# Retention stage of an eight-batch hybrid network: a ScalarE copy, a VectorE product and the key projection change places

## The reference, cut to what matters

```python
qkv = h @ weight_quant(qkv_w).T                 # q, k, v: 16 heads x 16
scores = einsum('bhtd,bhsd,hts->bhts', q, k, mask)   # mask: exp(-s*(t-s)), causal
o = 0.25 * einsum('bhts,bhsd->bhtd', scores, v)      # (chunked in the reference)
out = rmsnorm(rmsnorm(o) ) @ weight_quant(proj_w).T
x = x + out
```

## Time and profile before

| what | us |
|---|---|
| median of the runs | 1151.98 |
| lowest run | 1150.12 |
| profiled execution, its time | 1146.32 |
| profiled execution, its span | 1144.5 |
| PE busy in the span | 928.1 (81%) |
| DVE busy in the span | 703.6 (61%) |
| ACT busy in the span | 368.4 (32%) |

### The profile page before, as it was taken

The page is one execution under the profiler, slowest core; times in us unless marked ns, Lnnn a source line. Parts: engine busy times, 40 slices in busy tenths (PEclk is TensorE's granted clock), DMA queues, the critical chain, the costliest instruction groups (busy, mean ns, idle before and its releaser), DMA issues.

```text
span 1144.5 us, 21028 instructions
## 1 busy us (share of the span) xinstructions
PE 928.1 (81%) x8018; PEld 782.6 (68%) x8018; DVE 703.6 (61%) x1291; ACT 368.4 (32%) x663; POOL 320.1 (28%) x352
## 2 busy tenths in 40 slices
PE   3589987775886887778877999999668885699998
PEld 2466665454765776655655899997556664699998
DVE  4458876544577868788776545445676657454443
ACT  2126554331412321234332523233222222232222
POOL 4202221014845666321201104010044633330000
PEclk9669998686889998998887999999877878799999
DMA  8745541000011000355450000011454544210000
GB/s 220 231 126 154 156 117 44 2 1 10 19 56 47 1 1 1 112 170 153 127 166 14 1 2 1 1 44 41 89 96 87 110 84 74 37 20 19 11 20 19
DMA packets 148581, 76.78 MB, mean 67 GB/s; under 512 B 108993, under 2 KB 139713, under 8 KB 148481
## 3 DMA queue, kind: packets, MB, share of 16 engines
q1 hardware_dynamic: 139376, 65.47, 22.8%
q0 software_dynamic: 1424, 4.98, 1.5%
q10 hardware_dynamic: 7680, 4.98, 1.5%
HBM read 45.77 MB, written 29.36 MB: 66 GB/s over the span
## 4 chain that ended last, share of the span: by engine, by line
PE 56%; DVE 25%; issue 7%; ACT 5%; POOL 3%; SPq 2%; DMA 1%; DVEq 0%; ACTq 0%; POOLq 0%
PE SC L386 16%; PE pb L386 8%; PE OT L386 7%; DVE mx L1322 3%; PE OT L2154 3%; PE pa L386 3%; PE OT L1891 3%; PE SC L1844 3%; PE OT L2068 2%; PE SC L1873 2%; PE SC L2142 2%; PE pa L2337 2%; DVE pr L1575 2%; DVE m L1573 2%; DVE pr L1571 2%
## 5 line engine op out<-in xcount | busy, mean ns | idle before, releaser
L386 PE MATMUL SC<-xT_h,w_h 128*128 128x256 f32 x512 | 147.7, 289 | 13.8 <-DVE xT_l L1734 11.5
L386 PE MATMUL SC<-xT_l,w_h 128*128 128x256 f32 x512 | 146.1, 285 | 0.0
L386 PE MATMUL SC<-xT_h,w_l 128*128 128x256 f32 x512 | 145.3, 284 | 0.0
L386 PEld LDWEIGHTS SC<-xT_h,w_h 128*128 128x128 f32 x512 | 98.1, 192 | 17.0 <-DVE xT_l L1734 15.1
L1322 DVE TENSOR_REDUCE mx<-SC 128x4 f32<-128x1024 f32 x64 | 78.1, 1221 | 46.1 <-PE SC L1844 45.7
L386 PE MATMUL OT<-w,Qs 128*128 128x256 f32 x768 | 103.0, 283 | 2.3 <-DVE Qs L1744 1.4
L386 PEld LDWEIGHTS SC<-xT_h,w_l 128*128 128x128 f32 x512 | 98.2, 192 | 0.0
L386 PEld LDWEIGHTS OT<-w,Qs 128*128 128x128 f32 x768 | 95.2, 189 | 3.7 <-issue 2.1
L386 PEld LDWEIGHTS SC<-xT_l,w_h 128*128 128x128 f32 x512 | 97.7, 191 | 0.0
L1740 DVE TENSOR_TENSOR hidden_f<-SC,silu_gate 128x512 f32<-128x512 f32 x64 | 44.1, 689 | 84.5 <-ACT silu_gate L1202 84.5
L1744 DVE TENSOR_TENSOR Qs<-hidden_f,Qs 128x512 fp32r<-128x512 f32 x64 | 45.0, 703 | 44.7 <-ACT Qs L1210 44.7
(11 more groups left out here) (424 smaller groups left out, 2645.0 us busy)
## 6 DMA issues: line engine op xcount, KB each, us to landing
Qs<-q_stack SPq DMA_DIRECT2D x56, 128.0 KB, 2.8
k_stack<-KT_h SPq DMA_DIRECT2D x16, 256.0 KB, 2.6
k_stack<-KT_l SPq DMA_DIRECT2D x16, 256.0 KB, 3.1
q_stack<-QT_h SPq DMA_DIRECT2D x16, 256.0 KB, 2.2
q_stack<-QT_l SPq DMA_DIRECT2D x16, 256.0 KB, 2.8
o_groups<-b_O ACTq DMA_DIRECT2D x8, 512.0 KB, 2.9
Qs<-q_stack SPq DMA_DIRECT2D x56, 64.0 KB, 2.9
Ks<-k_stack SPq DMA_DIRECT2D x28, 128.0 KB, 3.2
```

The costliest lines, as they stand in the source:

```text
L386: ins = pe.matmul(out_ap, left[a], right[b], start=first and n == 0, stop=last and n == len(terms) - 1, **more)
```

## The change

On ACT, `x_high` goes from behind `squares`, `a_high` and the copies to the head of the round. On DVE, `a_low` goes from ahead of `masked` to behind `masked` and `x_low`. The key projection `k_out`, its high part `k_high`, its low part `low(b, KT, ...)` and its `store` each go one round later. Nothing is added or taken away, and no wait is changed.

```diff
@@ SP, narrow, at_slot
                                 for b in due(g, -12):
                                     store(b, "ql", "qstore", "qload", QT, q_dram)
-                                for b in due(g, -10):
+                                for b in due(g, -9):
                                     store(b, "kl", "kstore", "kload", KT, k_dram)
@@ ACT, narrow, at_slot
                     if ret:
+                        for b in due(g, -15):
+                            x_high(b)
                         for b in due(g, -8):
                             v_out(b)
...
                         for b in due(g, 26):
                             a_high(b)
-                        for b in due(g, -15):
-                            x_high(b)
                         for b in due(g, -13):
                             q_high(b)
-                        for b in due(g, -11):
+                        for b in due(g, -10):
                             k_high(b)
@@ DVE, narrow, at_slot
                     if ret:
-                        for b in due(g, 26):
-                            a_low(b)
                         for b, r in running(g, 0):
                             masked(b, r)
                         for b in due(g, -15):
                             x_low(b)
+                        for b in due(g, 26):
+                            a_low(b)
                         for b in due(g, -12):
                             low(b, QT, pb, "qh", "ql")
-                        for b in due(g, -10):
+                        for b in due(g, -9):
                             low(b, KT, pa, "kh", "kl")
```

## The result

The changed kernel takes 1140.51 us (median of four runs, 1134.99 to 1141.2) against 1151.35: a ratio of 0.9899, 95% interval 0.9859 to 0.9939, so 11 us or 1% less. The forecast was 1142. A few runs of the kernel before, of e4 and of e13 took 1231.97 us or more and are left out of the ratios. The run times go with the granted clock: of 56 later runs of the kernel before (1141.01 to 1159.82 us, median 1149.9), five with a mean clock of 0.885 took 1148.08 to 1150.26 us, and four at 0.893 took 1141.31 to 1141.71.

What follows compares the result with a forecast made beforehand. Neither engine is full; stalls between PE and DVE take 2.28 us a cycle. Gains 7.0 + 0 + 2.1 = 9.1 us off the profiled 1146.3 give 1137.2; 4.7 added for higher-lying runs gives 1142, range 1132 to 1154.

Steps and rivals of the forecast that it cites:

- Key projection: Retention cycles, rounds 5 to 7: moving it one round later gains 1.39 us a cycle, 7.0 in five; ends 0 and 11.4.
- residual stall: DVE before masked 7: the idle time shrinks from 1.76 to 0.36 us, since `k_out` now stands before round 7's scores.
- `store` and the loads: SP's queue: storing keys one round, about 2 us, later comes out of some 10 us of slack; cost nothing.
- One step of the layout: End of the laid-out cycle: `to_tokens` starts 0.28 us after `residual`, at 572.87; DVE is last, 574.46 against 575.85.
- The two orders: `x_high` ahead on ACT, `a_low` behind masked product on DVE: zero; ends 1.1 us gain, 2.8 loss.
- Clock: TensorE's granted clock in cycles 2 and 3: half of 4.24 us comes back, 2.1; ends 0 and 4.2.
- Lead-in and batch 0: Two key projections ahead of batch 0, among other layers' work: nothing, with ends of 0.9 us either way.
- What would show it: Changed profile: `k_out`'s 9.4 us wait, idle before masked 6 and `x_low`'s waits gone; full-clock cycles about 15.7 us; higher clock.
- The first: Rival, rounds 6 and 7: the stall only moves; gain 0 to 4 us, about 1150; chance 0.22.
- The second: Rival: DVE becomes the bound, all stalls go and the clock stays up; 15.6 us gain, 1135; chance 0.11.
- The third: Rival, `pa`'s rotation: late `x_turned` holds up `x_high`, `out_high` and round 2's `attend`; 10.6 us slower, 1162; chance 0.09.

Runs made afterwards that it cites:

- e4: Kernel before, with round 6's scores computed three more times ahead of `k_out` in cycles 1 to 5: 1139.09 us, ratio 0.9917.
- e13: e12 with `x_high` back in its old place, `a_low` still behind the masked product: 1138.64 us, ratio 0.992.
- e1: Kernel before with only the key projection, its copies and store one round later, both orders as before: 1142.74 us, ratio 0.995.
- e2: Kernel before with only `x_high` ahead and `a_low` behind, keys in their old round: median 1147.41 us, six runs from 1127.08 to 1150.87.
- e5: Kernel before with only the keys of batches 3 and later one round later, both orders as before: 1140.78 us, ratio 0.9911.
- e3: Changed kernel with the keys of batches 0 to 2 in their old round: 1136.37 us, ratio 0.9885.
- e12: The same kernel as e6, run again on another chip: 1126.95 us, ratio 0.9826.
- e11: Kernel before, unedited, profiled a second time on the same chip as e10: 1152.74 us, one run.
- e9: Kernel before with only `k_out` moved behind round 6's scores on PE; copies, low part and store as before: 1151.7 us, ratio 1.0026.
- e10: Changed kernel, unedited, profiled a second time on the same chip as e11: 1143.49 us, one run.
- e8: e3 with round 4's scores computed two more times ahead of `q_out` in cycles 3 to 5: 1131.44 us, ratio 0.9829.
- e6: Changed kernel with only the keys of batches 0 and 1 in their old round: 1126.72 us, ratio 0.9806.
- second pair: Second profiles of the changed kernel (e10) and the kernel before (e11), both unedited, on one chip: 1143.49 and 1152.74 us.

## Why the prediction came out as it did

The total held (1142 against 1140.51), in part by luck: the clock gave 5.7 us more than forecast, and the lead-in and batch 0 took 6.7 that the sum did not have. The two nearly cancelled.

**Key projection.** Right. Laid out at 1.39 us a cycle, it measured 1.37 alone (e1's cycle 3, at full clock). Taking it five times is a little much: between e2 and the changed kernel, at full clock in both, cycles 2 to 5 give 1.77, 1.50, 1.50 and only 0.51. The residual stall, laid out at 0.36 before masked 7, is 0.40. That `store` and the loads have the slack held: no scores wait for a load. One step of the layout counts unlike ends: `to_tokens` is set 0.28 us behind the recorded end of `residual` (573.32 for 0.74 us), while every other end is the start of what follows; with the recorded end the two chains come out within 0.01 us of each other, and the gain stays.

**The two orders.** Priced at nothing, with an end of 1.1 us of gain: mis-sized. In a full-clock cycle the price of nothing is nearly right: alone they give 0.1 us (e2), beside late keys 0.2 to 0.3 (15.53 against e1's 15.75, e5 against e3): with DVE busy 14.66 of 15.53 us there is little else that it waits for. Keys and orders together give 1.59 us, five times 8.0, an estimate on the high side. A second estimate goes by run times: a straight line through the 56 runs of the kernel before (6.7 us less for each 0.01 of mean clock, scatter 2.0 us) lies 6.8 us above the four runs of the changed kernel in the mean (2.7 to 8.4), 6.5 above e1's twelve and 2.1 above e2's six. So at like clock the keys give nearly all. But the clock is not alike: e13 and e12 differ in `x_high`'s place alone, and by 11 us.

**Clock.** Mis-sized, and hung on the wrong step. Cycles 1 to 5 of the profiles went from 89.7 to 76.1 us, 13.6; without the schedule's 8.0, 5.6 are the clock's. Cycle 6, with no key projection in it, gave 2.2 more (15.88 at 0.89, 13.72 at 1.00). That makes 7.8 us where I had taken 2.1 with an end at 4.2: I had counted only the two cycles that were slow in that profile against the third, and left out the clocks of 0.90 and 0.89 around them. And I had let the low stretch follow the stall. The granted clock of cycles 2, 3, 4 and 5 in all profiles:

| `x_high` | stall of round 5 | granted clock of cycles 2 to 5 |
|---|---|---|
| behind | there | before 0.81 0.75 1.00 0.90; e11 0.90 0.82 0.75 0.75 |
| behind | filled on PE | e4 0.81 0.91 0.91 0.91 |
| behind | gone or moved | e1 0.89 1.00 0.90 1.00; e5 1.00 1.00 0.90 0.90; e9 0.89 1.00 1.00 1.00; e13 0.89 0.82 0.90 0.90 |
| ahead | there | e2 1.00 1.00 1.00 1.00 |
| ahead | gone | after 1.00 1.00 1.00 1.00; e10 1.00 1.00 0.90 0.90; e3 and e8 1.00 1.00 1.00 1.00; e6 1.00 1.00 0.90 1.00; e12 1.00 1.00 0.90 0.90 |

With `x_high` at the head, cycles 2 and 3 have the full clock in all seven profiles, in e2 with the whole stall; behind, in 4 of 14 cycles. So the clock goes with the order that I had priced at zero at least as much as with the stall. Only e13 parts `x_high` from `a_low`, which stands behind the masked product in it too. By what way `x_high`'s place acts on the clock no run shows; each profile is one run, and e2's is of the faster group of its runs. The Trainium skill ("TensorE: Matmul & The Clock Gate", section "HAM oscillation — how this bites in real kernels") says that gaps pull the clock down. On this gap the traces are divided: with `x_high` behind, 7 of 16 cycles have the full clock where the stall is gone or moved and 1 of 8 where it is there, but e2 has it whole at 1.00, and e4 has it filled at 0.81 to 0.91. How much of the 7.8 the change itself brings stays open; the second pair gave the layer 17.5 us.

**Lead-in and batch 0.** I had put the two projections ahead of batch 0 at "nothing, with ends of half a stall (0.9) either way", and the one in batch 0 had no term. Lead-in and batch 0 took 1.7 and 5.0 us in the first pair; in the second the lead-in took 4.3, and batch 0 came out shorter than before (18.21 at 0.91 against 19.26 at 0.82). At like clock the projections stay inside the old end: batch 0 costs 0.9 us at 1.00 and 0.2 at 0.82, and a lead-in with early keys, 33.2 us at 0.95 and 35.57 at 0.86, would take some 34.5 at 0.90 by an estimate between the two, against 34.9 with late keys. What they cost is plain in batch 0: PE's share of the other layers' work stands in the same round and queue, the moved `k_out` came on top of it ahead of the scores, and DVE waits 1.59 us at full clock and 4.29 at half. The rest of the 6.7 came with a clock of 0.90 for 0.95 and 0.69 for 1.00, and my sum let the clock only rise. Whether the moved projections bring that clock is open: e2 and e11, with early keys, have 0.82 in batch 0, and e3, e4, e5, e8, e9 and before have 1.00.

**What would show it.** `k_out`'s wait, the idle time before masked 6 and `x_low`'s waits went as said; full-clock cycles are 15.53 where I said 15.7. The clock of the first profile is higher in cycles 2, 3, 5 and 6 and level in 1 and 4; e10 has 0.90 in cycles 4 and 5 (16.97 and 16.99 us).

**Rivals.** The first, a stall that only moves, is what e9 built: it comes when the copies stay, not here. The second, DVE as the bound, is nearer than I gave it (94% busy in a full-clock cycle). The third does not occur: `x_high` waits 6.6 us in five rounds at their head, with the copy behind it, and still no `attend` waits for ACT. What the prediction takes from the Trainium skill for it, that ScalarE and VectorE are strict first-in-first-out, stands in "TensorE: Matmul & The Clock Gate" under "Architectural detail: the array is 16× 32×32, not 1× 128×128", not in the section named there.

**Rest of the difference.** Of the 11.3 us between the profiled spans, 2.8 lie in code that the change doesn't touch (4.5 less ahead, 1.7 more behind); in the second pair that code went 4.0 the other way. They are no effect that I can claim.

## What to carry to other kernels

A step that waits at the head of an in-order queue costs what stands behind it, so lay one cycle out again from the timeline rows; that gave the gain of a full-clock cycle to 0.02 us. Move its copies with it, or the wait reappears at them. Then lay the first batches out too: there the moved step can meet another layer's work in its new round, and a guard on the batch number leaves those few where they were. At like clock that was worth some 1 us here. And don't price an order by its waits alone: moving one copy ahead was priced at some 1 us in all by its waits and was worth 11 us in the runs (e13 against e12). Compare cycles at the same granted clock before giving a difference to the schedule.

## What the runs showed of the hardware

Two layers behind retention, with code that no kernel changed, came in two sizes. In the profiles of e2, e4, e6, e12 and e13 they take 358.5 to 360.3 us, the sixth layer at a granted clock of 1.00 and the seventh at 0.81 or 0.82. In both of before, both of after, and e1, e3, e5, e8 and e9, they take 366.4 to 369.4, at 0.97 or 0.98 and 0.78 or 0.79. It came back the same in each of the three kernels that were profiled twice (before, after, e6 as e12), which speaks for the kernel but does not rule out chance: three pairs are few, each profile is one run, and the six runs of e2 alone lie in two groups, at 1127.08 to 1129.6 and 1145.26 to 1150.87 us. The profile of e3 was of the larger size and that of e6, one key projection away, of the smaller; so was e4's, with three extra scores a cycle. What sets it I could not find: it goes neither with the layer's length (122.1 us in e6, 122.5 in e3) nor with the stall (there in e4, gone in e12). Some 6 to 11 us, about as much as the change itself, hang on it.
